# Attention weights times the normalised input, projected afterwards, in a four-layer graph network kernel

## What is computed

```python
x = _layernorm(x + L0(x))   # gated neighbour sums
x = _layernorm(x + L1(x))   # graph convolution, two linear maps, two batch norms
x = _layernorm(x + L2(x))   # graph attention, below
x = _layernorm(x + L3(x))   # two graph convolutions, then four LSTMs over windows of 1 to 4 nodes

def L2(h):                                  # adj_matrix is adj
    Wh = einsum('bnf,fo->bno', h, W)
    s1, s2 = Wh @ a1, Wh @ a2
    e = s1[:, :, None] + s2[:, None, :]
    e = where(e >= 0, e, 0.2 * e)
    e = where(adj_matrix[None] == 0, -inf, e)
    return einsum('bij,bjo->bio', softmax(e, axis=-1), Wh)

def L3(x):
    h = relu(einsum('ts,bsh->bth', adj, x @ Wg0 + bg0))
    h = relu(einsum('ts,bsh->bth', adj, h @ Wg1 + bg1))
    for p in 1..4:      # an LSTM over windows of p nodes; its last state replaces the window's last node
        ...
```

## Time and profile before

| | |
|---|---|
| median of 3 runs | 692.0 us (691.77 to 692.42) |
| profiled execution, its own time | 690.08 us |
| its span, first to last instruction | 688.3 us |
| mean granted TensorE clock | 0.990 of 2.4 GHz |
| busy TensorE / its weight loads | 646.6 us (94%) / 444.6 us (65%) |
| busy VectorE / ScalarE / GpSimd | 459.1 us (67%) / 405.5 us (59%) / 250.8 us (36%) |
| first matmul of slots 2, 3, 4, 5 | 202.94, 262.4, 323.93, 385.43 us |

### The profile page before, as it was taken

How to read it: one execution, slowest core, us unless ns; L and a number is a source line. 1 busy time by engine, 2 the same in 40 slices (tenths; PEclk the granted TensorE clock), 3 DMA queues, 4 the chain that set the end, 5 groups by cost and what they waited for, 6 DMA issues and landing times.

```text
span 688.3 us, 9196 instructions
## 1 busy us (share of the span) xinstructions
PE 646.6 (94%) x2818; PEld 444.6 (65%) x2818; DVE 459.1 (67%) x1338; ACT 405.5 (59%) x819; POOL 250.8 (36%) x250
## 2 busy tenths in 40 slices
PE   8899988997899999999999999999999999998993
PEld 6656645445675686578568757855875685575573
DVE  5988876677965567757766775777577665454444
ACT  3668675956735665674476557555745665445552
POOL 4789881005741113430443343043224403400301
PEclk9999999999999999999999999999999999999997
DMA  9223000000000000000000000000000000000000
GB/s 352 88 105 153 1 1 1 0 0 1 2 0 1 1 0 2 0 31 1 1 32 1 0 1 30 1 2 30 1 0 1 32 0 1 31 1 0 32 0 31
DMA packets 4225, 16.75 MB, mean 24 GB/s; under 512 B 464, under 2 KB 464, under 8 KB 4048
## 3 DMA queue, kind: packets, MB, share of 16 engines
q1 hardware_dynamic: 4176, 16.16, 6.1%
HBM read 11.97 MB, written 4.19 MB: 23 GB/s over the span
## 4 chain that ended last, share of the span: by engine, by line
PE 51%; DVE 15%; ACT 7%; POOL 7%; issue 5%; DVEq 0%; ACTq 0%; POOLq 0%
PE QQ L747 18%; PE QQ L759 11%; POOL X L473 4%; PE PA L730 4%; PE QQ L624 4%; ACT raw L1008 2%; ACT raw L1001 2%; PE PB L721 2%; DVE STL L1159 2%; POOL RSD L378 2%; PE PB L711 2%; DVE HB L1306 2%; PE PA L702 2%; PE PA L692 2%; DVE raw L1398 2%
## 5 line engine op out<-in xcount | busy, mean ns | idle before, releaser
L1001 ACT ACTIVATE raw<-QQ,BL 128x256 f32<-128x256 f32 (+2 forms) x312 | 166.1, 563 | 98.6 <-PE QQ L759 71.4
L747 PE MATMUL QQ<-HT,WT 128*128 128x256 f32 (+2 forms) x624 | 206.0, 474 | 7.3 <-DVE HT L1406 3.9
L747 PEld LDWEIGHTS QQ<-HT,WT 128*128 128x128 f32 x624 | 116.2, 190 | 74.3 <-issue 33.3
L378 POOL TENSOR_TENSOR RSD<-VAR,pw 128x8 f32<-128x8 f32 (+1 forms) x36 | 54.1, 1502 | 294.1 <-DVE VAR L1181 294.1
L759 PE MATMUL QQ<-HB,WT 128*128 128x256 f32 (+2 forms) x384 | 114.7, 441 | 2.2 <-DVE HB L1406 1.9
L1388 DVE SCALAR_TENSOR_TENSOR raw<-raw 128x512 f32<-128x512 f32 (+2 forms) x88 | 50.2, 570 | 80.8 <-ACT raw L1001 80.8
L759 PEld LDWEIGHTS QQ<-HB,WT 128*128 128x128 f32 x384 | 69.5, 190 | 34.0 <-issue 12.4
L1008 ACT ACTIVATE raw<-raw 128x512 f32<-128x512 f32 (+2 forms) x88 | 45.2, 513 | 45.3 <-DVE raw L1398 35.0
L492 POOL TENSOR_TENSOR HB<-HB 128x512 f32<-128x512 f32 x28 | 35.1, 1271 | 80.6 <-ACT HB L965 80.6
L1406 DVE SCALAR_TENSOR_TENSOR HB<-raw 128x256 f32<-128x256 f32 (+2 forms) x48 | 24.0, 499 | 29.4 <-ACT raw L1008 29.4
L1406 DVE SCALAR_TENSOR_TENSOR HT<-raw 128x512 f32<-128x512 f32 (+2 forms) x40 | 24.3, 608 | 27.8 <-ACT raw L1008 27.8
(11 more groups left out here) (180 smaller groups left out, 1067.6 us busy)
## 6 DMA issues: line engine op xcount, KB each, us to landing
raw<-in_xt SPq DMA_DIRECT2D x8, 512.0 KB, 6.1
four<-in_x SPq DMA_DIRECT2D x8, 512.0 KB, 4.9
out<-four SPq DMA_DIRECT2D x7, 512.0 KB, 2.6
WT<-in_lstm SPq DMA_DIRECT2D x1, 2048.0 KB, 9.3
later<-in_later SPq DMA_DIRECT2D x1, 662.0 KB, 8.7
AD<-in_adj SPq DMA_DIRECT2D x1, 512.0 KB, 4.9
out<-four SPq DMA_DIRECT2D x2, 256.0 KB, 2.1
early<-in_early SPq DMA_DIRECT2D x1, 274.0 KB, 2.9
```

What stands on the lines that cost most here:

```text
L378: pool.tensor_tensor(RSD[kk][:, ts], VAR[kk][:, ts], pw[:, ts], ALU.pow).then_inc(ln[k]["rstd"], some)
L747: mm = pe.matmul(steps_view(Q[q], k), WT[:, 0, (p - 1) * 4 + q, :], ht_view(par, k), start=True, stop=(s == 0))
L1001: act.activation(TG[q][:, 0:n], Q[q][:, 0:n], ACT.Tanh, scale=0.5 if q == G else 0.25, bias=BL[:, p - 1, q:q + 1]).then_inc(g_ok, 1)
```

## The change

Six things change together.

1. For groups 2 to 7 attention is reordered: the weights multiply X2 (a_mix, 256 columns), ScalarE copies the product (a_mixed), and W is applied afterwards (a_project_mix). a_turn, a_scores, a_project and their copies go, for these groups. The denominators come from the accumulator of the exponentials (accum_out) and one reciprocal (a_inverse).
2. s1 and s2 come from VectorE: 16 dot products of 128 columns per group (a_dots), of the sum before the norm with two centred rows of W a1 and W a2, scaled by a_s12. TensorE spreads s2 over the rows by 8 transposes of a broadcast column (a_rows). The rows are made once (four small VectorE operations, two TensorE products in place of two warming ones).
3. The third norm is taken by halves, and GpSimd scales each half after its power, at the end of the slot instead of at the next one's start.
4. ScalarE's gates wait for the reader of their own buffer, not for the hidden state of the step before (lstm_gates).
5. The orders of a slot change on all engines: TensorE's a_spread0 is split around x(2); x(3), h(3) and a_rows stand ahead of a_weigh0. On VectorE t_norm comes ahead of a_biased0, and a_apply1 behind cell(5).
6. The constants that are loaded later grow by 127 columns.

```diff
@@ GpSimd, slot
             def slot(s, par, A, B, L, T):
-                if B:
-                    scale2(s - 1)
                 if A:
                     rstd(1, 0, s)
...
                     scaled(s + 2)
-                    rstd(2, 1, s)
+                    for h in range(2):
+                        rstd(2, 1, s, h)
+                        scale2(s, h)
@@ TensorE, before the second product
             pe.wait_ge(gate_z, GROUPS)
-            spin(Q[3][:, 0:P], 14)
+            for k in range(2):
+                mm = pe.matmul(Q[3][:, k * P:(k + 1) * P], AR[:, k * P:(k + 1) * P], WTR, start=True, stop=True)
+            spin(Q[3][:, 2 * P:3 * P], 12)
@@ TensorE, new
+            def a_rows(g):
+                pe.wait_ge(s12_ok, g - 1)
+                reach(pe, sp_ok, 2 * g)
+                for b in range(GB):
+                    for c in range(NC):
+                        t = 2 * b + c
+                        mm = pe.transpose(turned(PA, c, b), S12[:, 1, t:t + 1].broadcast_to([P, P]), ident[:])
+                mm.then_inc(s2_ps, 2)
+            def a_mix(g, some):
+                pe.wait_ge(ln[1]["out"], TILES * (g + 1))
+                f = front(g)
+                for b in some:
+                    pe.wait_ge(pt_ok, GB * g + b + 1)
+                    for m in range(NC):
+                        mm = pe.matmul(f.AB[b][:, 0:NODES], turned(X2, m, b), f.MS[:, 2 * b + m, :],
+                                       start=(m == 0), stop=(m == NC - 1))
+                    mm.then_inc(px_ps, 1)
+            def a_project_mix(g, some):
+                f = front(g)
+                for b in some:
+                    pe.wait_ge(px_ok, GB * (g - 2) + b + 1)
+                    for c in range(NC):
+                        at = NODES + c * P
+                        mm = pe.matmul(f.AB[b][:, at:at + P], turned(f.X2T, c, b), WX[:, 0:P], start=True, stop=True)
+                    mm.then_inc(att_ps, 1)
@@ TensorE, a_weigh1 and a_spread1
-                pe.wait_ge(max_ok, upto(g + 2) * TILES) if g else None
...
-                pe.wait_ge(wh_ok, upto(g + 2) * NC) if g else None
+                pe.wait_ge(max_ok, upto(g + 2) * TILES) if g else None
@@ TensorE, slot
                 x(1)
                 t_turn(s - 3, 1 - par) if T else None
-                a_spread0(s - 1) if B else None
+                a_spread0(s - 1, (0, 1)) if B else None
                 x(2)
+                a_spread0(s - 1, (2, 3)) if B else None
+                x(3)
+                h(3)
+                a_rows(s) if A else None
                 a_weigh0(s - 1) if B else None
-                x(3)
-                a_turn(s) if A else None
-                h(3)
-                if A:
-                    a_project(s, 0)
-                    a_scores(s)
-                    a_project(s, 1)
                 x(4)
                 x(5)
...
                 a_turn_e(s, range(GB)) if A else None
                 h(8)
                 x(9)
-                a_attend(s, (0, 1, 2)) if A else None
+                if A:
+                    a_mix(s, (0, 1, 2))
+                    a_project_mix(s, (0, 1))
                 h(9)
                 x(10)
-                a_attend(s, (3,)) if A else None
+                if A:
+                    a_mix(s, (3,))
+                    a_project_mix(s, (2,))
                 h(10)
+                a_project_mix(s, (3,)) if A else None
@@ ScalarE
+            def a_mixed(g, some):
+                f = front(g)
+                for b in some:
+                    act.wait_ge(px_ps, GB * (g - 2) + b + 1)
+                    act.activation(f.X2T[:, b * NODES:(b + 1) * NODES], f.AB[b][:, 0:NODES], ACT.Copy).then_inc(px_ok, 1)
...
-                        e = act.activation(f.E1[:, t], f.E1[:, t], ACT.Exp, bias=f.EB[:, t:t + 1], scale=SLOPE)
+                        e = act.activation(f.E1[:, t], f.E1[:, t], ACT.Exp, bias=f.EB[:, t:t + 1], scale=SLOPE,
+                                           accum_out=DEN[:, t:t + 1] if g > 1 else None)
...
-                    reach(act, h_ok, j)
+                    if q == O:
+                        reach(act, h_ok, j)
+                    elif q == F or STEPS[k - 1][1] > 0:
+                        reach(act, cf_ok if q == F else ca_ok, FORGETS[NSTEP] * g + FORGETS[k])
+                    else:
+                        reach(act, cell_ok, j)
@@ ScalarE, slot
                 cell(0)
                 cell(1)
+                cell(2)
                 a_spread(s - 1) if B else None
-                cell(2)
-                a_turned(s) if A else None
+                cell(3)
                 a_relu(s - 1) if B else None
-                gates(3)
-                a_projected(s, 0) if A else None
-                state(3)
-                a_projected(s, 1) if A else None
...
                 cell(8)
+                a_mixed(s, (0, 1, 2)) if A else None
                 cell(9)
+                a_mixed(s, (3,)) if A else None
                 cell(10)
@@ VectorE, new
+            def a_dots(g):
+                dve.wait_ge(z1_ok, 2 * (g + 1))
+                dve.wait_ge(rows_ok, 1)
+                for k, junk in enumerate((one_a, one_c)):
+                    for t in range(TILES):
+                        dve.tensor_tensor_reduce(nth(junk, t), nth(Z, t), WAR[:, k], 1.0, 0.0,
+                                                 ALU.mult, ALU.add, DOT[:, k, t:t + 1]).then_inc(dots_ok, 1)
+            def a_s12(g):
+                dve.wait_ge(dots_ok, 2 * TILES * (g - 1))
+                dve.wait_ge(ln[1]["rstd"], 2 * (g + 1))
+                dve.tensor_tensor(S12[:], DOT[:], RSD[0][:].unsqueeze(1).broadcast_to([P, 2, TILES]), ALU.mult).then_inc(s12_ok, 1)
@@ VectorE, slot
                 cell(2)
-                a_apply1(s) if A else None
+                if A:
+                    a_dots(s)
+                    a_s12(s)
+                t_norm(s - 3) if T else None
                 a_biased0(s - 1) if B else None
-                t_norm(s - 3) if T else None
                 cell(3)
                 a_max(s) if A else None
                 cell(4)
                 a_bias(s) if A else None
                 cell(5)
+                a_apply1(s) if A else None
                 a_biased1(s - 1) if B else None
...
                 cell(8)
                 if A:
                     a_weights(s, (2, 3))
-                    a_sum2(s, (0, 1, 2))
+                    a_inverse(s)
+                    a_sum2_mix(s, (0, 1))
                 cell(9)
                 if A:
-                    a_sum2(s, (3,))
-                    a_stats2(s)
+                    a_norm2(s, 0)
+                    a_sum2_mix(s, (2, 3))
                 cell(10)
-                a_small2(s) if A else None
+                a_norm2(s, 1) if A else None
```

More of the change, by code:

```diff
@@ L166, in build @@
         WA2 = sb("WA2", [P])
+        WAR = sb("WAR", [2, P])
+        WAM = sb("WAM", [2])
+        DOT = sb("DOT", [2, TILES])
+        S12 = sb("S12", [2, TILES])
+        DEN = sb("DEN", [TILES])
         BL = sb("BL", [SKIPS, 4])
@@ L521, in _ @@
             rstd(2, 2, 1, 1)
+            scale2(1)
             slots(slot)
@@ L548, in vectors @@
                 pe.wait_ge(later_ok, 16)
-                pe.matmul(Q[2][:, 0:P + 1], WTR, AR, start=True, stop=True).then_inc(setup_pe, 1)
+                pe.matmul(Q[2][:, 0:P + 1], WTR, AR[:, P - 1:2 * P], start=True, stop=True).then_inc(setup_pe, 1)
             def gates(g):
@@ L622, in output1 @@
                     reach(pe, out2_ok, 2 * (g - 2) + q + 1)
+                    pe.wait_ge(rows_ok, 1) if (g, q) == (1, 1) else None
                     for h in range(HC):
@@ L639, in a_residual, with a_turn @@
                 mm.then_inc(y_ps, size(h))
-            def a_turn(g, h=None):
+            def a_turn(g, h):
                 pe.wait_ge(ln[1]["out"], TILES * g + tls(h).stop)
-                reach(pe, sp_ok, 2 * before(g))
                 for b in batches(h):
@@ L647, in a_turn, with a_scores, a_project @@
                 mm.then_inc(x2t_ps, size(h))
-            def a_scores(g, h=None):
+            def a_scores(g, h):
                 pe.wait_ge(x2t_ok, halves(g, h))
-                reach(pe, y0_ok, 2 * before(g))
                 f = front(g)
-                for q in range(2) if h is None else [h]:
-                    mm = pe.matmul(f.PB[:, q * BANK:(q + 1) * BANK], WA2[:], f.X2T[:, q * BANK:(q + 1) * BANK],
-                                   start=True, stop=True)
-                mm.then_inc(s2_ps, size(h))
-            def a_project(g, c, h=None):
-                if c or h:
+                pe.matmul(f.PB[:, h * BANK:(h + 1) * BANK], WA2[:], f.X2T[:, h * BANK:(h + 1) * BANK],
+                          start=True, stop=True).then_inc(s2_ps, 1)
+            def a_project(g, h):
+                if h:
                     pe.wait_ge(wh_ok, 2 * g + 1)
                 pe.wait_ge(x2t_ok, 2 * (g + 1))
```

(37 more changed lines are left out.)

52 lines of the change are left out of this document (21 added, 31 removed).

## The result

| | before | after |
|---|---|---|
| median of the runs, us | 692.2 | 748.3 (747.56 to 748.85, 4 runs) |
| ratio to before, 95% interval | | 1.081 (1.079 to 1.082) |
| span of the profiled execution, us | 688.3 | 746.0 |
| mean granted clock of TensorE | 0.990 | 0.952 |
| TensorE / VectorE / ScalarE / GpSimd busy, us | 646.6 / 459.1 / 405.5 / 250.8 | 657.4 / 494.3 / 408.4 / 256.2 |

Slower, as forecast, but by 56 us and not by 30: 748.3 lies above the range (706 to 733). TensorE, with 1.84 us less to do per slot, is busy for 10.8 us longer, and its mean granted clock is lower (0.952 for 0.990): part of its work ran at the lower clock.

A forecast was written before the change was run, and what follows sets the result against it. TensorE was taken to bound slots 2 to 7. The profiled 690.1 + 18 (slots, mainly the new wait) + 10 (clock) + 2 (accumulator reads) gave 720.1, or 722 us on the median's scale; range 706 to 733.

The forecast's parts named there:

- The order up to x(4): Slot start to LSTM step 4's input product: cell(3) queued behind a_biased0, TensorE idle 5.1 us, x(4) +1.3 us later.
- The wait at a_spread0: Early in the slot, TensorE reaches a_spread0 at 7.0 us and waits 0.9 us for VectorE's a_sum1.
- Sixteen dot products at 0.21 apart: VectorE, after cell(2): the 16 dots take 3.4 us in all, so a_rows need not wait.
- cell(10) at 0.8: VectorE at the slot's start: cell(10) begins at about 0.8 us, after two sums following the last attention projection.
- From x(4) on: Rest of the slot: old order, 19.73 us to the turning; a_apply1 some 0.2 late but covered; TensorE's work then grows 1.66.
- rival 4: Worse: clock at half over 3.4 us per slot, or dots and accumulator reads at their upper costs; 735 us, chance 0.12.
- the clock at x(4): TensorE's clock falls in or after each gap, costing x(4) and x(5) 1.7 to 1.8 us; +10 us over six slots.
- an accumulator read: ScalarE's exponentials: 0.08 us per read, only the last four delaying the last turning; +0.33 us a slot, 2 in all.
- The tail, +1.66: TensorE after the turning: mixes and projections replace attention products, 3.46+1.78-3.58, adding 1.66 us a slot.
- the mixes' copies on ScalarE: After the turning: four copies of 0.42 us each lie under TensorE's next product; uncovered, one would cost about 0.7.
- 1 (the clock holds): The same new wait before x(4), but without a fall of the clock: 712 us, chance 0.16.
- 2 (faster): cell(3) is not held up for long, TensorE's work alone sets the slot at 59.4 us: 678 us, chance 0.08.

The follow-up runs named there:

- Experiment 4: Kernel after with VectorE's a_biased0 moved behind cell(3) instead of ahead of it: 711.1 us.
- Experiments 1 and 2: Kernel after, one edit each: a_apply1 directly behind a_s12, 726.6 us; GpSimd's weight sums cut to 8 of 256 columns from group 2 on, 725.0 us.
- experiment 3: Kernel after with 18 products of ones filling TensorE's idle time between a_weigh0 and x(4) in the six attention slots: 733.3 us.
- experiment 8: Kernel 7 without the exponentials' accumulator sums, the denominators set to one: 689.4 us.
- kernel 7: Kernel after, reordered: a_biased0 behind a_bias, a_apply1 behind the first a_weights, fourth norm behind cell(5), ScalarE's relu and GpSimd's tail moved; 693.0 us.

## Why the prediction was right and wrong

- **The order up to x(4): right.** a_weigh0 done at 23.8 and x(4) at 28.9 after the slot's start were forecast; 367.41 (365.70 plus 1.88, less the tail of 0.17) and 372.51 less 343.61 are 23.80 and 28.90. The wait at a_spread0 came out at 0.75 for 0.9. Sixteen dot products at 0.21 apart and cell(10) at 0.8 (0.73) also stood. In the slot shown the idle time is 4.93 by TensorE's row, 5.10 from the last product's modelled end. Experiment 4 shows the queue order as the cause: one line moved, and the gap shrinks.
- **The step that failed** is in "From x(4) on": a_apply1, "some 0.2 late, and TensorE has the product h(6), 2.3 us (8 of 340 columns) before it needs that bias". Its 2.14 us were taken from a place where GpSimd was idle, and moved to one where GpSimd adds weights. It takes 5.03 there, 2.9 more. h(6)'s 2.3, less the 0.2 and the bias's own 1.2, would have covered 0.9 of that; the rest is the 2.08 of idle time at a_spread1 in each of six slots (12.5), and in four of them the clock falls as well (7.4 of busy time): 19.9 us. Experiments 1 and 2 give 21.7 and 23.3 back. The prediction had the evidence in hand, a 1873 ns operation beside GpSimd's, and used it for the dots alone, in rival 4, not for the other VectorE work that the change moves. The 0.84 of cell(6) in the slot itself it did not see.
- **Mis-sized: the clock at x(4).** The mechanism was right (granted clock 0.50 behind the gap), but a fall costs 2.1 to 2.9 us, not 1.7: 15 for 10 (experiment 3), and slot 8's gap has a seventh, 1.6. The price came from a single row of another shape; the six rows here spread over 0.8 us.
- **Right in size: an accumulator read**, 0.08 taken and 0.09 measured. How many count is less sure. Only the last four were charged (0.33 a slot); in the slot shown the turning takes 2.46 for 1.94, 0.52 more, and experiment 8 gives 0.3 to 0.9 a slot, in kernel 7's order. The Trainium skill (ScalarE: Activation LUTs, What ACT_TABLE_LOAD costs) gives 186 ns with 93 of overlap for an ACTIVATE; it does not speak of the accumulator's read, but the rows of that read show nearly the same: 0.19 each, 0.09 of it effective.
- **The tail, +1.66, and the mixes' copies on ScalarE: right.** From the turning to the next slot there are now 16.34 us (414.24 less 397.90) and 14.16 stood before, 2.18 more. 0.52 of that lies in the turning (waits for ScalarE), and the rest is 1.66.
- **Rivals.** 1 (the clock holds) fell: every one of the six gaps has its fall. 2 (faster) named the right lever: with the gap gone and no collision the time is 681.6 (after five moves in three queues), where it gave 678. 4 (735) was the nearest, with its mechanism put at the wrong operation. The range ended below it. Its lower end was also added up wrongly: a gap a microsecond shorter in six slots is 6 us and not 4.

The sum with these two terms set right: 722 + 19.9 + 5.9 = 747.8, against 748.3. Both were read from the trace afterwards, so that is an account and no second forecast; small errors in the other terms may cancel.

## What to carry to other kernels

When an operation of VectorE is moved, look at GpSimd's timeline at the new place before taking its duration along: 8 columns can cost a microsecond there. In hand-written queue orders (the fixed order of instructions on each engine), ask of each bias or copy that is inserted which recurrent chain is queued behind it; the chain's owner goes first. A change that cuts the bounding engine's work can be right and still lose; reordering alone took this one from 748.3 to 681.6.
